# A graph network on one core: fewer signals from TensorE, and an extra product of 512 constant columns per tile

## The reference

```python
def spmm(h):                                   # first layer, used twice
    msg = h[src] * edge_w[:, None]
    agg = segment_sum(msg, dst, num_segments=N)
    return agg + self_w[:, None] * h
h = spmm(x @ W1 + b1)
h = relu(batch_norm(h))
x = layernorm(x + spmm(h @ W2 + b2))
# second layer: attention over the edges, 8 heads of 16
scores = einsum('ehd,ehd->eh', q[row], k[col]) / 4 + edge_emb @ eb_w.T + eb_b
attn = exp(scores - seg_max[row]) / (seg_sum[row] + 1e-10)
out = segment_sum(attn[..., None] * v[col], row) @ out_w.T + out_b
x = layernorm(x + out)
```

## Time and profile before

| what | value |
|---|---|
| median of 3 runs | 11755.06 us (11748.66 to 11759.41) |
| span of the profiled execution | 11509.7 us |
| TensorE busy | 7087.3 us, 62%, 39548 products |
| VectorE busy | 5806.8 us, 50% |
| GpSimd busy | 6063.8 us, 53% |
| ScalarE busy | 2519.6 us, 22% |
| mean granted TensorE clock | 0.694 |

### The profile page before, as it was taken

The page is one execution under the profiler, slowest core; times in us unless marked ns, Lnnn a source line. Parts: engine busy times, 40 slices in busy tenths (PEclk is TensorE's granted clock), DMA queues, the critical chain, the costliest instruction groups (busy, mean ns, idle before and its releaser), DMA issues. The chain is left out here.

```text
span 11509.7 us, 203325 instructions
## 1 busy us (share of the span) xinstructions
PE 7087.3 (62%) x39548; PEld 6173.5 (54%) x39549; DVE 5806.8 (50%) x16002; ACT 2519.6 (22%) x8525; POOL 6063.8 (53%) x6650
## 2 busy tenths in 40 slices
PE   6687878777566566666666644444444446773774
PEld 5576777777455555555555523333333335662664
DVE  7433333333355455555555554444444445668777
ACT  8100000000122222222222210000000003442885
POOL 6465655555544444444443465555555555553665
PEclk8655555565656666666666667777777778996997
DMA  1233333333311111111111132222222225552553
GB/s 37 76 87 81 85 85 82 85 84 83 103 35 32 32 33 32 31 32 32 32 31 31 32 83 84 88 87 85 86 88 85 84 85 146 137 138 58 154 154 103
DMA packets 1057786, 868.49 MB, mean 75 GB/s; under 512 B 214824, under 2 KB 950424, under 8 KB 1057736
## 3 DMA queue, kind: packets, MB, share of 16 engines
q0 software_dynamic: 179664, 437.87, 12.6%
q1 hardware_dynamic: 643032, 319.49, 10.5%
q10 hardware_dynamic: 235040, 110.58, 3.4%
HBM read 578.04 MB, written 287.84 MB: 75 GB/s over the span
## 5 line engine op out<-in xcount | busy, mean ns | idle before, releaser
L1492 POOL DMA_INDIRECT spmm_rows<-h_table,spmm_index_ring x3136 | 3082.1, 983 | 3130.5 <-PE bank L1569 2099.5
L1569 PE MATMUL bank<-spmm_rows,spmm_hot 128*128 x6660 | 2067.8, 412 | 550.2 <-DVE region_ab L1542 440.3
L1845 POOL DMA_INDIRECT kv_sorted<-expand_payload,expand_where_ring x1568 | 1508.9, 962 | 1114.3 <-issue 1066.1
L1569 PEld LDWEIGHTS bank<-spmm_rows,spmm_hot 128*128 128x128 f32 x6660 | 1620.1, 296 | 641.8 <-issue 623.5
L1866 PE MATMUL bank<-region_ab,expand_hot_t 128*128 x3336 | 1097.8, 486 | 1392.6 <-DVE expand_hot_t L1884 1121.2
L1542 DVE TENSOR_TENSOR region_ab<-region_ab,bank 128x128 f32 x3330 | 957.7, 288 | 1873.3 <-remote 902.8
L1866 PEld LDWEIGHTS bank<-region_ab,expand_hot_t 128*128 128x128 f32 x3336 | 775.4, 245 | 1577.1 <-issue 1451.3
L1901 DVE SCALAR_TENSOR_TENSOR expand_payload<-expand_payload,region_c,bank 128x256 f32 x1668 | 801.6, 481 | 1236.3 <-issue 397.3
L745 PE MATMUL bank<-spmm_beside_hot_hi,spmm_beside_hot_lo 128*128 128x98 bf16 x1568 | 563.1, 359 | 1044.5 <-ACT spmm_beside_next_slot L782 818.8
L782 ACT COPY spmm_beside_next_slot<-bank 128x98 f32<-128x98 f32 x1568 | 379.0, 242 | 2690.6 <-PE bank L745 1296.6
L704 DVE CUSTOM_DVE_ANT_0 spmm_beside_junk<-bank,spmm_beside_hot_hi 128x98 f32<-128x98 f32 x1568 | 448.1, 323 | 959.4 <-DMA bn_cols<-in_L_gnn_bn_var_dram 690.4
(11 more groups left out here) (353 smaller groups left out, 12601.3 us busy)
## 6 DMA issues: line engine op xcount, KB each, us to landing
score_k_rows<-kv_sorted SPq DMA_DIRECT2D x420, 288.0 KB
mix_mixed<-kv_sorted SPq DMA_DIRECT2D x420, 256.0 KB
spmm_beside_attr_sb<-in_edge_attr_dram ACTq DMA_DIRECT2D x390, 256.0 KB
spmm_rows<-h_table,spmm_index_ring POOLq DMA_INDIRECT x3136
kv_sorted<-expand_payload,expand_where_ring POOLq DMA_INDIRECT x1568
kv_sorted<-spmm_beside_blank SPq DMA_DIRECT2D x1, 15232.0 KB
kv_sorted<-spmm_beside_blank SPq DMA_DIRECT2D x98, 136.0 KB
h_table<-region_ab SPq DMA_DIRECT2D x28, 448.0 KB
```

Of the source, the lines that this page charges most:

```text
L1492: nc.gpsimd.indirect_dma_start(rows[:, h * HALF + k, :], None, table, bass.IndirectOffsetOnAxis(ap=index_ring[:, h, k:k + 1], axis=0)).the ...
L1569: last = nc.tensor.matmul(sums_of(k), hot[:, k // HOTS % HOT_GROUPS, k % HOTS, :], tile_of(rows, place[k % HALF]), start=True, stop=True)
L1845: nc.gpsimd.indirect_dma_start(kv_sorted, bass.IndirectOffsetOnAxis(ap=where_ring[:, h, k:k + 1], axis=0), payload[:, h * HALF + k, 0:ROW] ...
```

## The change

- `CountUpto` (beside the first product): the counting products L514 signal once for eight columns instead of once for each; VectorE waits by eighths accordingly.
- Both sparse products: the sums lie four tiles in a bank (`SUMS = 4`) instead of two. TensorE signals at the end of each four, VectorE adds four at once, and TensorE waits for the additions of the four that are two back.
- Expansion: `made` is signalled once per group of four tiles instead of once per pair, and VectorE waits for the whole group.
- `keep_busy`: before TensorE waits for a tile's rows (both products) or for a group's matrices (expansion, four times), it multiplies 512 constant columns of bf16 by zeros, into a bank that nothing else uses. Nothing reads the result.
- `until_window` and `pairs_done`, the rows that the sequencers load numbers from, become unsigned 16-bit integers.

```diff
+        def keep_busy(into):
+
+            nc.tensor.matmul(into[:, 0:512], zeros_bf[:, 0:P], iota_rows[:, :, :].rearrange("p a b -> p (a b)")[:, 0:512], start=True, stop=True)
...
                 if k % HALF == 1:
-                    need(dve, self.used, c - 1)
+                    need(dve, self.used, q - 1)
...
                 if k % HALF == 4:
-                    need(dve, self.used, c - 4)
+                    need(dve, self.used, q - 1)
...
-                nc.tensor.matmul(bank[0][0:NT, 0:P], self.highs[:, h, :, j], self.upto[:, h, :, j], start=False, stop=False).then_inc(self.used, 1)
+                counted = nc.tensor.matmul(bank[0][0:NT, 0:P], self.highs[:, h, :, j], self.upto[:, h, :, j], start=False, stop=False)
+                if j == HALF - 1:
+                    counted.then_inc(self.used, 1)
...
+                SPARE_BANK = 3 if name == "spmm1" else 5
+                SUMS = 4
...
-                    return bank[6 + k // 2 % 2][:, k % 2 * D:(k % 2 + 1) * D]
+                    return bank[6 + k // SUMS % 2][:, k % SUMS * D:(k % SUMS + 1) * D]
...
-                                if k % 2 == 0 and k < tiles - 1:
+                                if k % SUMS < SUMS - 1 and k < tiles - 1:
                                     continue
                                 dve.wait_ge(summed, t + 1)
-                                for m in range(k - k % 2, k + 1):
+                                for m in range(k - k % SUMS, k + 1):
...
-                            if k % 2 == 0:
-                                need(pe, added, t - 2)
+                            if k % SUMS == 0:
+                                need(pe, added, t - SUMS)
+                            keep_busy(bank[SPARE_BANK])
                             pe.wait_ge(arrived, until[k % HALF])
...
-                            if k % 2 == 1 or k == tiles - 1:
-                                last.then_inc(summed, 1 + k % 2)
+                            if k % SUMS == SUMS - 1 or k == tiles - 1:
+                                last.then_inc(summed, 1 + k % SUMS)
...
+                        for m in range(GROUP):
+                            keep_busy(bank[6])
                         pe.wait_ge(hot_ready, g + 1)
...
-                            if m % 2 == 1:
-                                last.then_inc(made, 2)
+                        last.then_inc(made, GROUP)
...
-                            if m % 2 == 0:
-                                dve.wait_ge(made, t + 2)
+                            if m == 0:
+                                dve.wait_ge(made, t + GROUP)
```

More of the change, by code:

```diff
@@ L4 @@
 from concourse import mybir
-F32, I32, BF16 = mybir.dt.float32, mybir.dt.int32, mybir.dt.bfloat16
+F32, I32, BF16, U16 = mybir.dt.float32, mybir.dt.int32, mybir.dt.bfloat16, mybir.dt.uint16
 ALU, ACT, AX = mybir.AluOpType, mybir.ActivationFunctionType, mybir.AxisListType
@@ L143, in gnn @@
         node_d, node_s = node_rows[0:1, :], node_rows[S_ROW:S_ROW + 1, :]
-        until_window, window_place = node_rows[UNTIL_ROW:UNTIL_ROW + 1, :], node_rows[PLACE_ROW:PLACE_ROW + 1, :]
-        pairs_done = sb("pairs_done", [1, E_HALVES], I32)
+        until_wide, window_place = node_rows[UNTIL_ROW:UNTIL_ROW + 1, :], node_rows[PLACE_ROW:PLACE_ROW + 1, :]
+        until_window = until_wide.bitcast(U16)[:, 0:S_TILES]
+        pairs_done = sb("pairs_done", [1, E_HALVES], U16)
         fill_tile = sb("fill_tile", [1, NT], I32)
@@ L194, in gnn @@
         breaks = region_c[:, 0:CHUNK_LEN // 2 + 1].bitcast(BF16)
-        node_at, steps_row = until_window, node_d.bitcast(BF16)[:, 0:S_TILES]
+        node_at, steps_row = until_wide, node_d.bitcast(BF16)[:, 0:S_TILES]
         sum_places = window_place
+        def keep_busy(into):
+            nc.tensor.matmul(into[:, 0:512], zeros_bf[:, 0:P], iota_rows[:, :, :].rearrange("p a b -> p (a b)")[:, 0:512], start=True, stop=True)
         def column(flat):
@@ L493, in vector_step @@
             def vector_step(self, dve, i, k):
-                c, q, h = i * TURN + k, 2 * i + k // HALF + 1, (k // HALF + 1) % 2
+                q, h = 2 * i + k // HALF + 1, (k // HALF + 1) % 2
                 if k % HALF == 1:
-                    need(dve, self.used, c - 1)
+                    need(dve, self.used, q - 1)
                     self.compare(self.highs[:, h, :, :], self.hi, q, NT, ALU.is_equal, self.highs_ready)
                 if k % HALF == 4:
-                    need(dve, self.used, c - 4)
+                    need(dve, self.used, q - 1)
                     self.compare(self.upto[:, h, :, :], self.lo, q, P, ALU.is_ge, self.upto_ready)
```

## The result

The changed kernel takes 12057 us (12047 to 12067, four runs), the one before in the same set 11757 (11749 to 11760). That is 1.0258 times, with a 95% interval of 1.0243 to 1.0272: slower by 300 us, where the forecast was 445 us faster.

A forecast was written before the change was run, and what follows sets the result against it. Bound: GpSimd's gathers plus late TensorE signals, and TensorE at half clock between them. -175 - 80 + 10 - 180 - 20 = -445 us: span 11509.7 to 11065, plus 245 carried, 11310 us; range 10750 to 11800.

The forecast's parts named there:

- (c): Extra 512-column product, all three stages: raises TensorE's clock; 0.43 us each at half clock, 0.22 at full, hidden there.
- +10 us: Second product: net cost of the extra product, 11.9 us per eight columns against 11.8 before.
- rival Q: From product_8cols, not the prediction: one more instruction per tile or bank written delays TensorE's signals; 1.02 to 1.03 times before.
- The clock: TensorE's granted clock rises to 0.8 to 0.9 in first product and expansion, about 0.75 in second product.
- The signals: Fewer stalls on late TensorE signals: first product -175 us, second -80, expansion -180, tails -20.
- (b): Ring of sums grows from four to eight tiles: TensorE runs further ahead; GpSimd learns of windows one tile later on average.
- The 16-bit rows: Count rows loaded by the sequencers, half as wide as before: given no gain or loss.
- Rival 3: Slower: after stalls the product runs at half clock where TensorE must catch up; about 12300 us, 11%.
- Rival 2: Fewer signals save nothing, lateness belongs to GpSimd's run of gathers, only the clock helps; 0 to -100, 11705 us, 20%.
- Rivals 1 and 4: 1: signals were the whole matter, 10600 us, 14%. 4: clock doesn't answer to the product, 12800 us, 5%.
- Rival 1: First product and expansion run at GpSimd's pace: -575 - 500 - 80 = -1155, 10600 us, 14%.
- The carried 245 us: Median of runs, 11755.06 us, above the profiled span, 11509.7; added unchanged to the forecast span of 11065.

The follow-up runs named there:

- product_b: Changed kernel with finer signals restored (counts per column, sums and expanded rows per two tiles), 512-column product and 16-bit rows kept; late signals: 11907 us, 1.0309 times before.
- rows16_b: Changed kernel with everything undone but the 16-bit rows, in a set with late signals: 11593 us, 1.0046 times before.
- signals_b: Changed kernel without the 512-column product in any stage, in a set with late signals: 11549 us, 0.9834 times before.
- signal_by_two: Changed kernel, but TensorE signals its sums per two tiles; bank and VectorE's additions stay by four; late signals: 12095 us, 1.0288 times before.
- more_signals: Changed kernel without the product, plus six TensorE signals per eight columns that nobody awaits, in both sparse products; punctual signals: 9572 us, 1.0335 times before.
- sums_of_four: Changed kernel with only sums per four tiles and 16-bit rows left; no product, other signals fine again; punctual signals: 9580 us, 1.0349 times before.
- rows16_only: Changed kernel with everything undone but the 16-bit rows, in a set with punctual signals: 9359 us, 1.0115 times before.
- gpsimd_by_four: As product_b, but GpSimd rounds its two awaited counts up to fours, two register operations each; late signals: 12247 us, 1.0421 times before.
- rows32_product: Changed kernel with finer signals restored, product kept, count rows in 32 bits with a mask per loaded value; punctual signals: 9283 us, 1.0025 times before.
- rows32_masked: Changed kernel without product or coarser signals, count rows in 32 bits with a mask per loaded value; punctual signals: 9351 us, 1.0101 times before.
- product_8cols: As product_b, but the extra product has 8 columns instead of 512; late signals: 12112 us, 1.0316 times before.

## Why the prediction was wrong

**The step that failed** is (c), the price of the product: "at full clock the extra product hides under GpSimd or VectorE", +10 us in the second product and nothing in the others. Single durations were right, 0.21 to 0.24 us at full clock (forecast 0.22) and 0.43 at half. What was wrong is how many of them run at half clock, and on the path. The prediction's sum for the second product had 2.3 columns of eight at half clock. In product_b, where all 4998 are on record, 40% of them last 550 ns or more (nearly all the rest last under 400) in the first sparse product, 48% in the second, 14% in the expansion. The measured price of the term is 2.6 to 4.2% of the time, 300 to 500 us, where +10 us stood. The windows of both kernels in one late set, rows16_b and then product_b, each with first product, second product, expansion:

```profile
430.00:2950.00 2520.00, 1985.58 (x9493) 1883.13 (x9492) 964.21 (x2609) 228.68 (x390) 1523.81 (x1528) 0.58 0.31 83
3150.00:6650.00 3500.00, 2178.34 (x12451) 1909.95 (x12451) 1769.20 (x7010) 801.70 (x3104) 1434.75 (x1480) 0.63 0.12 32
7000.00:9500.00 2500.00, 1207.77 (x4711) 908.00 (x4709) 1028.58 (x1965) 102.14 (x557) 1425.58 (x1482) 0.73 0.23 85
```

```profile
430.00:3000.00 2570.00, 2077.34 (x11117) 1835.93 (x11116) 963.55 (x2605) 228.78 (x391) 1516.21 (x1531) 0.77 0.30 81
3150.00:6650.00 3500.00, 2294.21 (x13417) 1957.12 (x13417) 1688.52 (x6696) 769.99 (x2980) 1377.44 (x1420) 0.72 0.13 34
7200.00:9700.00 2500.00, 1380.77 (x6096) 932.16 (x6096) 995.71 (x1903) 99.09 (x540) 1381.97 (x1441) 0.79 0.23 83
```

Divide TensorE's busy time by gathers and take eight: 10.40 us become 10.85, 11.77 become 12.93, 6.52 become 7.67. Divide the stretch likewise: 13.19 become 13.43, 18.92 become 19.72, 13.50 become 13.88. The clock rose in all three, gave back less than the product took, and from a third to seven tenths of the difference shows in the period. In the first and second product this account fits in sign and size. In the expansion it fits for 512 columns and not for 8: there the short products add nothing to TensorE's busy time (6.52 us per eight scatters) and the stage is 2798 us against 2683 (rows16_b's 2637 carried over by the sets' 1.7%). What else an extra product costs there is not settled; later signals (rival Q) are one candidate.

**The clock** was expected at 0.8 to 0.9 in the first product and the expansion and is 0.71 and 0.77; 0.75 was right for the second (0.72). In the rows read above it stands at half behind a late signal's stall (0.43 us for the product at 4994.93, 3.78 for the eight at 8508.58), and the catch-up starts there. With punctual signals the same kernel holds 0.92, 0.84 and 0.95, and the product's loss is small: the forecast's clock belongs to a kernel without the stalls.

**The signals** were to give 455 us (the sum's 445 has the product's +10 in it). signals_b gives 1.7%, about 195, but not where forecast. Against rows16_b carried over, the first product gains nothing (2618 for 2626; forecast 175), the expansion next to nothing (2668 for 2683; 180), and the second 168 us (3555 for 3723; 80), with hardly fewer signals. That looks like (b), the ring of eight tiles, but the runs don't bear it out. By the profile TensorE waited only 41 us for VectorE's additions in the second product without the ring. What shrinks is its wait for ScalarE's copy, which itself waits for TensorE's signal. The first two lines are rows16_b, the third signals_b (engine, line, waited for: us in total, times, longest):

```profile
PE bank L751 <- ACT spmm_beside_next_slot L788: 696.7, 232, 6.3
PE bank L1577 <- DVE region_ab L1550: 41.0, 14, 7.9
```

```profile
PE bank L752 <- ACT spmm_beside_next_slot L789: 312.6, 186, 4.4
```

And signal_by_two, which has the ring and the finer signals, is 81 us longer in the second product than the change. So the ring alone isn't shown to be the gain. Which part of the change pays there stays open: more_signals was to tell and landed in a punctual set. The other half of (b), that GpSimd hears of a finished window a tile later, I named and gave no price: all of the sums by four together come to 2.3% in a punctual set (sums_of_four over rows16_only), and the later count alone to 1.1% in late ones (gpsimd_by_four over product_b).

**The 16-bit rows** at nothing were off by 50 us late, 100 punctual. "No row shows such a load" was true, and a bound was owed: the rows of before had the 32-bit load.

**The rivals.** Rival 3 had mechanism and sign right: slower, the product right behind the stalls at half clock. Its figure, 12300, missed 12057 by 243 us, and its threshold was wrong: it was to decide below a clock of 0.65 in the second product, and it decided at 0.72. A better test, an estimate, can be had from the product's own two prices: TensorE's other work must fall by what the product adds. Per eight columns of the second product that is 8.5 products x 0.33 us (48% at 0.43, the rest at 0.24) = 2.8; the other work fell by 11.77 - (12.93 - 2.8) = 1.6. Rival 2, fewer signals save nothing, holds for the first product and the expansion. Rivals 1 and 4 fell: GpSimd still stalls, and the clock did answer. Rival 1's sum also takes 500 us for an expansion whose bound the text puts at 620.

**The named checks.** GpSimd's wait in the first product was to be under 300 us and is 484. Four L1912 in a row: yes. L1579's pairs at half their time: no, 349 ns for 412, the mean of one product on the two pages. Second stage within 150 us: 117 more, so this passed and told nothing. Late signals still there: yes. What the text named last as the thing that would upset all, lateness that depends on what TensorE does, doesn't show in the second product (1091 us for 1092) and can't be excluded in the expansion.

**The carried 245 us.** The profile of before spans 11510, its runs 11755. In one late set before ran at 11513 to 11578, in the others at 11726 and above; the profiled execution most likely came from a set like the first; that is a guess from its length. It would make the traces' +536 us, and with them the longer stages above, overstate the change, which the runs put at 300.

**Best versions.** In a late set signals_b is 1.7% faster than before and, by the ratios of two sets, 4.1% faster than the change. In a punctual one nothing here beats before; rows32_product comes within 0.25%. No version beats both kernels in both.

## What to carry to other kernels

An engine's clock is not a gain by itself. Price work that is only there to raise the clock at its half-clock duration, ahead of the first result after each stall, and compare TensorE's busy time per unit of work, not the clock. A product made short is not a product without cost: look at what its neighbours take before you use it as a control. Coarser signals can give a longer ring and a later go for whoever counts; price both, for each waiter. Before a gain is built on a wait that looks like delivery and not like work, time the kernel in more than one set of runs: here three sets of seven didn't have that wait, and the order of the versions was another in them.

## What the runs showed of the hardware

- The same program took 9254 to 9267 or 11543 to 11757 us depending on the set, and waiters of TensorE started 0.1 us or some 5 us behind it while GpSimd issued indirect DMAs. In the second product 20% of ScalarE's copies started over 1 us late in rows16_b, none of 1567 in rows16_only, the same kernel.
- A register load of eight 16-bit values took 1.9 us on TensorE's queue (rows16_b), of eight 32-bit ones 0.59 (rows32_masked).
- With a product of 8 columns ahead of each sum (product_8cols) the granted clock of the second sparse product was 0.50, for 0.63 without it (rows16_b). The pair behind it took 0.57 us at half clock, for 0.43 behind a product of 512 columns (product_b), and a product of the sum 491 ns for 407 in rows16_b.
